# A graph network on one core: the block stage's loop on VectorE in another order, with two places per register load, and five moves around the last layer

## The reference

```
x = layernorm(x + L0(x, edges))          # h = x + sum of neighbours; relu(h W1 + b1) W2 + b2
x = layernorm(x + L1(x, src, dst))       # two layers of relu(h Ws + mean of neighbours Wn + b)
x = layernorm(x + L2(x, W, bias, edge_weight, src, dst))   # relu(segment_sum(edge_weight * (x W)[src], dst) + bias)
x = layernorm(x + L3(x, src, dst, edge_attr_20, edge_weight, edge_attr_3, ...))
```

## Time and profile before

| | us |
|---|---|
| median of 3 runs (2280.93 to 2287.22) | 2282.07 |
| the profiled execution's own time | 2290.75 |
| its span, first to last instruction | 2288.8 |
| block stage, first to last add | 396.1 to 707 |
| last product of L2 to first `filter_out` product | 1284 to 1317.8 |

### The profile page before, as it was taken

One profiled execution on the slowest core, in us unless ns is written; L12 is line 12 of the kernel. 1 busy time (PEld: TensorE's weight loads), 2 busy tenths in 40 slices (PEclk: granted clock), 3 DMA queues, 4 the chain that ended last, 5 costly groups with the idle time before them and its releaser, 6 DMA issues.

```text
span 2288.8 us, 37510 instructions
## 1 busy us (share of the span) xinstructions
PE 2078.5 (91%) x7867; PEld 1177.4 (51%) x7867; DVE 1595.2 (70%) x4611; ACT 1146.1 (50%) x3291; POOL 1237.1 (54%) x1526
## 2 busy tenths in 40 slices
PE   4787797888888999999999799999999999999987
PEld 3443343566664545455444555555555555555545
DVE  8976668898986070110413488888888888888886
ACT  0476456787872010000010366666666666666654
POOL 1477881000004888888886266666666666666541
PEclk9698798766668999999999899999999999999999
DMA  5410320000002121121121133333333333333321
GB/s 195 156 15 3 88 70 16 0 0 0 0 0 62 38 44 21 20 62 21 19 54 23 63 93 98 100 100 100 98 97 97 98 98 101 99 101 97 98 76 45
DMA packets 74566, 146.96 MB, mean 64 GB/s; under 512 B 26317, under 2 KB 37058, under 8 KB 74119
## 3 DMA queue, kind: packets, MB, share of 16 engines
q0 software_dynamic: 44192, 95.61, 16.9%
q1 hardware_dynamic: 28764, 47.76, 6.3%
q10 hardware_dynamic: 1538, 2.72, 0.3%
HBM read 123.11 MB, written 22.36 MB: 64 GB/s over the span
## 4 chain that ended last, share of the span: by engine, by line
PE 78%; DVE 13%; issue 4%; ACT 2%; DVEq 1%; another core or an unknown queue 1%; DMA 0%; ACTq 0%; POOL 0%; SPq 0%; POOLq 0%
PE ps L914 24%; PE ps L657 11%; PE ps L676 8%; PE ps L805 5%; PE ps L748 4%; PE ps L852 4%; PE ps L897 3%; PE ps L899 3%; PE ps L898 3%; PE ps L900 3%; DVE adj_t L1249 2%; PE ps L804 2%; PE ps L771 2%; DVE dense L1440 1%; DVE dense L1439 1%
## 5 line engine op out<-in xcount | busy, mean ns | idle before, releaser
L914 PE MATMUL ps<-adj_t 128*128 128x512 f32 x1288 | 614.7, 599 | 14.0 <-DVE adj_t L1677 14.0
L1132 ACT ACTIVATE adj_t<-adj_t 128x128 f32<-128x128 f32 x966 | 315.4, 389 | 210.0 <-DVE adj_t L1656 204.2
L590 POOL DMA_INDIRECT adj_t<-z_table,adj_t x322 | 310.5, 964 | 153.9 <-DVE adj_t L1666 68.3
L914 PEld LDWEIGHTS ps<-adj_t 128*128 128x128 f32 x1288 | 231.3, 189 | 248.7 <-issue 214.5
L548 POOL DMA_INDIRECT src_table<-st_two,src_rows x216 | 261.6, 1211 | 70.4 <-issue 65.2
L534 POOL DMA_INDIRECT pair_table<-dense x176 | 215.3, 1223 | 126.4 <-issue 115.8
L805 PE MATMUL ps<-dense 128*128 128x128 f32 x832 | 245.8, 414 | 0.0
L541 POOL DMA_DIRECT2D st_two<-records x54 | 31.9, 591 | 353.3 <-DVE adj_t L1464 353.1
L676 PE MATMUL ps<-wring,dense 128*128 128x512 f32 (+1 forms) x480 | 210.0, 600 | 4.5 <-issue 3.2
L897 PE MATMUL ps<-dense_r 128*128 128x512 f32 x322 | 200.2, 622 | 2.5 <-POOL dense_r L598 2.5
L1464 DVE TENSOR_TENSOR adj_t<-adj_t,ps 128x256 f32 x416 | 171.2, 411 | 30.8 <-issue 28.8
(11 more groups left out here) (285 smaller groups left out, 3775.0 us busy)
## 6 DMA issues: line engine op xcount, KB each, us to landing
src_table<-dense SPq DMA_DIRECT2D x8, 656.0 KB, 6.6
adj_t<-z_table,adj_t POOLq DMA_INDIRECT x322, 3.5
records<-dense SPq DMA_DIRECT2D x1, 5000.0 KB
adj_t<-src_table SPq DMA_DIRECT2D x73, 64.0 KB
adj_t<-zeros SPq DMA_DIRECT2D x1, 4576.0 KB
src_table<-st_two,src_rows POOLq DMA_INDIRECT x216
st_two<-records POOLq DMA_DIRECT2D x54, 62.5 KB
adj_t<-zeros SPq DMA_DIRECT2D x1, 3328.0 KB
```

Source lines behind the costliest of these rows:

```text
L590: g.indirect_dma_start(out=zg[:, s, c, :], out_offset=None, in_=z_table, in_offset=bass.IndirectOffsetOnAxis(ap=dsti[:, s, c:c + 1].bitcas ...
L914: last = mm(bank[6 + h], oh[:, c, :], msg[:, c, h * D:(h + 1) * D], start=c == c0, stop=c == c0 + count - 1)
L1132: last = A(msg[:, c, (2 + k) * P:(3 + k) * P], msg[:, c, MSG:MSG + P], ACT.Copy, scale=side[:, s, c, C_Y - ATT + k:C_Y - ATT + k + 1])
```

## The change

- Block stage on VectorE: `half` becomes `turn`. For each place the add comes first and the `select` for the chunk eight later behind it. Both waits (`blk_done`, `blk_added`) stand ahead of the add. A register load with two values comes ahead of the add of every even place, so four loads per turn of 8 places in place of one. The loop keeps its 50 turns.
- GpSimd clears `agg` when all ten tiles of `residual("l2_agg")` are done, not when the last product is.
- VectorE prepares L3's weights ahead of `residual("l2_agg")`; only the copy `identb` and the fill of `stat`, which lie in space that is still in use, stay behind it.
- ScalarE loads the table for exp and ln ahead of the copies of z.
- The ten stores of z are issued by SyncE, behind its record loads for the first two groups.
- GpSimd's `hidden_lo(0, 0)` stands behind two of the first four gathers, not behind all four.

```diff
@@ sync
             load_group(0, 0)
             load_group(0, 1)
+            for t in range(NT):
+                sp_eng.wait_ge(done["l3_z"], t + 1)
+                sp_eng.dma_start(z_table[t * P:t * P + rows_of(t), :], xb[0:rows_of(t), t, :]).then_inc(z_out, 16)
@@ gpsimd
-            pool.wait_ge(full, first["l2_agg"] + NT)
+            pool.wait_ge(done["l2_agg"], NT)
             g.memset(agg, 0.0).then_inc(agg_zero, 1)
             split(0, 0)
             split(0, 1)
-            for c in range(GROUP):
-                gather(0, 0, c)
+            gather(0, 0, 0)
+            gather(0, 0, 1)
             hidden_lo(0, 0)
+            gather(0, 0, 2)
+            gather(0, 0, 3)
@@ scalar
             copies_T("l3_xT")
+            nc.scalar.preload_act_table_set("natural_log_exp_and_others")
             for t in range(NT):
                 A(xb[0:r, t, :], taken("l3_z", t)[0:r, :], ACT.Copy).then_inc(done["l3_z"], 1)
-                act.wait_ge(done["l3_z"], t + 1)
-                act.dma_start(z_table[t * P:t * P + r, :], xb[0:r, t, :]).then_inc(z_out, 16)
...
             act.wait_ge(l3w_ready, 2)
-            nc.scalar.preload_act_table_set("natural_log_exp_and_others")
@@ vector, block stage
-            def half(i, h, first=False, last=False):
...
+            def turn(i, tail=False):
+                n0 = i * PLACES
+                for k in range(PLACES):
+                    c, n = k % (2 * AB), n0 + k
+                    if k % 2 == 0:
+                        _, block_at = nc.values_load_multi_w_load_instructions(
+                            pair_offs[0:1, ds(n, 2)], engines=[mybir.EngineType.DVE], min_val=0, max_val=AW_COLS - P, ...)
+                    dve.wait_ge(blk_done, n + 1)
+                    if not (isinstance(n, int) and n == 0):
+                        dve.wait_ge(blk_added, n)
+                    a = adj[:, :, ds(block_at[k % 2], P)]
+                    v.tensor_tensor(a, a, bank[c][:, 0:2 * P].rearrange("p (k n) -> p k n", k=2), ALU.add).then_inc(blk_added, 1)
+                    if not tail or k < PLACES - 2 * AB:
+                        select(n + 2 * AB, c)
+
+            for c in range(2 * AB):
+                select(c, c)
+            turn(0)
+            with dve.Fori(1, PAIR_CHUNKS // PLACES - 1) as i:
+                turn(i)
+            turn(PAIR_CHUNKS // PLACES - 1, tail=True)
@@ vector, towards L3
             residual("l1b_out", 48, relu=True)
-            residual("l2_agg", 64, relu=True)
...
-            link(v.tensor_copy(identb, ident[:, :]))
             row = pcol[0:PRODUCTS * ATT, :]
...
             link(v.scalar_tensor_tensor(bf2_r, bf2_r, ident[:, 0:1], bf2_lo, ALU.mult, ALU.add))
+            residual("l2_agg", 64, relu=True)
+            link(v.tensor_copy(identb, ident[:, :]))
             v.memset(stat, 1.0).then_inc(l3w_ready, 1)
```

More of the change, by code:

```diff
@@ L380, in build @@
         AB_IT = PAIR_CHUNKS // (2 * AB)
+        PLACES = 2 * AB
+        assert PAIR_CHUNKS % PLACES == 0
         L3_LOADS = 8 + 2 * PRODUCTS
@@ L1433, in _, with select @@
             dve.wait_ge(pair_merged, 3)
-            def select(i, c):
-                n = i * (2 * AB) + c
+            def select(n, c):
                 col = n * PAIR_COLS + PAIR_AT
@@ L1440, in select @@
                 v.tensor_scalar(sel_b[:, c, 1, :], iotab[:, :], dense[:, ds(col + 1, 1)], None, ALU.is_equal).then_inc(sel_ready, 1)
-            block_at = []
-            def half(i, h, first=False, last=False):
[L1446 to L1455, removed]
-                            skip_runtime_bounds_check_because="a sum of some of the steps between blocks; all of them make the last block's place")
[L1457 to L1478, removed]
+            def turn(i, tail=False):
[4 more added lines that the diff above has]
+                        _, block_at = nc.values_load_multi_w_load_instructions(
+                            pair_offs[0:1, ds(n, 2)], engines=[mybir.EngineType.DVE], min_val=0, max_val=AW_COLS - P,
+                            skip_runtime_bounds_check_because="a sum of some of the steps between blocks; all of them make the last block's place")
+                    dve.wait_ge(blk_done, n + 1)
[5 more added lines that the diff above has]
+                        select(n + 2 * AB, c)
```

## The result

Measured side by side on one chip, the kernel after takes 2360.55 us (median of 5 runs, 2354.93 to 2363.11), the kernel before 2284.74 (5 runs, 2280.93 to 2287.22). The ratio is 1.033, interval 1.0311 to 1.0349: slower by 76 us. The forecast was 2368, the range 2320 to 2402.

What follows compares the result with a forecast made beforehand. VectorE was taken to bound the block stage, its sequencer's time paid in full. +94 us for the loop, +2 for the turns outside and -10 behind L2 made +86: 2282 to 2368 us, range 2320 to 2402.

Steps and rivals of the forecast that it cites:

- Two take 0.30 + 0.04 = 0.34: Block stage, VectorE: a two-value register load takes 0.34 us, from one value at 0.30 and eight at 0.60.
- The load costs 0.82 - 0.16 = 0.66 us each turn. The branch costs 0.10 more: Block loop of the kernel before: of each turn's idle time the eight-value load costs 0.66 us, the branch 0.10.
- Each load costs 0.40: Block loop: each two-value load adds 0.40 us between S2, the step before the add, and the add.
- 0.15 for the waits: Block loop: the two waits ahead of the add cost 0.15 us at each of four even places, bounds 0 and 0.15.
- The branch, 0.37: Block loop: no longer beside the turn's last add, the branch costs 0.37 us a turn; lower bound 0.10.
- the 0.02 at odd places: Block loop: at the four odd places the waits cost 0.02 us each, bounds 0 and 0.05.
- TensorE under 70 of 100 us busy: Block stage, a sign to look for: TensorE under 70 of 100 us busy in the profile after.
- Behind L2, -10.4: From L2's end to L3's filter: the moves bring the first filter product 10.4 us earlier, bounds -12 and -5.
- A: Block stage: loads cost less than added, no extra wait instruction or a hidden branch; 2319 to 2352 us, chance 0.24.
- B: Block stage: loads have a floor, each costing what the eight-value one does; 2422 us, chance 0.07.
- C: Block stage: VectorE's sequencer runs ahead, loads and waits vanish under adds and selects; 2234 us, chance 0.07.
- D: Half-hidden loads, 0.1 us each, even out with the 10 us behind L2; 2275 to 2289 us, chance 0.02.

Runs made afterwards that it cites:

- run 1: Kernel after with one value per register load, so eight loads a turn: 2387.84 us, ratio 1.0448 to the kernel before.
- run 2: Kernel after with four values per register load, so two loads a turn: 2287.63 us, ratio 1.0014 to the kernel before.
- run 9: Kernel after, still four loads a turn, each loading four values of which two are used: 2363.87 us, ratio 1.0452 to the kernel before.
- run 10: Kernel after, still four loads a turn, each loading three values of which two are used: 2382.57 us, ratio 1.0533 to the kernel before.
- Run 4: Kernel after with the order and waits of the kernel before (select, load, add), still two values per load: 2336.73 us, ratio 1.0227 to the kernel before.
- run 3: Kernel after with the wait for the product moved ahead of the preceding `select`: 2335.77 us, ratio 1.0223 to the kernel before.
- run 7: Kernel before with only the late clearing and the early weights: 2272.19 us, ratio 0.9959 to the kernel before.
- run 8: Kernel before with only the late clearing, weights left behind the normalised tiles: 2283.24 us, ratio 1.0001 to the kernel before.
- Run 6: Kernel before with all five moves behind L2, block stage untouched: 2272.04 us, ratio 0.9958 to the kernel before.
- run 12: Kernel after with 32 places a turn, loads of four values, the order of the kernel before: 2233.34 us, ratio 0.9873 to the kernel before.

## Why the prediction was right, and where it was not

- **Direction, place and size: right.** +86 forecast on the profiled execution, +72.5 found; the slower time, the block stage as its place, four idle spells a turn with the one at the branch longest, 208 loads.
- **"Two take 0.30 + 0.04 = 0.34": wrong.** This is the term that failed, though the 0.53 lies inside its bounds of 0.30 and 0.60. A straight line was laid between one value and eight, but eight is two aligned fours. Measured 0.53, shown by the trace after; that the line between one and eight does not hold is shown by runs 1, 2, 9 and 10. By itself the true length would have added 4 x 0.19 x 50 = 38 us, which makes 2406 of the forecast, outside the range. That the forecast came so near is thus partly luck.
- **"The load costs 0.82 - 0.16 = 0.66 us each turn. The branch costs 0.10 more": wrong split.** Run 4 has, in the order of before, loads with the branch ahead of them and loads without: the branch costs 0.29, the load its own length less 0.12. The 0.76 of before is 0.48 for the load and 0.28 for the branch. "The sequencer is hardly one instruction ahead" described one place, not a rule: in the kernel after the load starts 0.12 us before S2.
- **"Each load costs 0.40", and 0.15 for the waits: right as a sum, by two errors that cancel.** The forecast from S2 to the add was 0.06 until the load starts, 0.34 for it, 0.31 behind it, 0.71 together. Measured: -0.12, 0.52, 0.29, together 0.69. The second wait ahead of the add costs 0.12 at an even place (runs 3 and 4) and 0 at an odd one, inside the bounds.
- **The branch, 0.37:** measured 0.30. That, and the 0.02 at odd places and at each load, make up the turn of 7.70 against 7.9, and with 50 turns most of the 85.5 against 96.
- **"TensorE under 70 of 100 us busy": wrong,** 76.7. There are 313 matmuls for 402; at the 0.211 us each of before they would fill 66 us. That they would run at 1.2 GHz from 415 us to the stage's end, and take 0.245, was not seen. It bounds nothing there: odd places still follow after 0.66 us.
- **Behind L2, -10.4: right,** -10.1. L1483 is never over 0.6 us, z runs at 0.91 us a tile at 2.4 GHz (forecast 0.85), the last copy ended 14.7 us behind L2's last tile (14), the filter came after 23.6 (24). Preparing the weights cost nothing, and "`identb`, then under the clearing, waits until 1296.3" did not come, for it ran just ahead of the clearing; nothing hung on it. Runs 7 and 8 add that the late clearing brings its gain only with the weights moved out of its way. Run 6, which has the moves alone, is 0.42% faster than before: the change contains a gain of 10 us and a loss of 85.
- **The rivals.** A (2319 to 2352) did not come: the EVENT_SEMAPHORE and the ALU_OP are there, and the branch is not hidden. B had some truth in that two values are dearer than the line says, but a floor it is not: one value takes 0.30 us and four 0.344. The Trainium skill's page "DMA: Bandwidth & Descriptors" (section "Latency and other measured facts") gives `tensor_load` about 600 ns at least; these loads from SBUF on VectorE go down to 0.297, so here the measurement decides against it. C (2234): the load starts only 0.12 us ahead of S2, not the 0.5 named, and nothing vanishes. The depth that the Trainium skill's page "TensorE: Matmul & The Clock Gate" (section "Architectural detail: the array is 16× 32×32, not 1× 128×128") gives for VectorE's queue does not show in this loop, whose sequencer waits for the last add once a place: its wait starts 0.04 us after that add's end at the places without a load. D did not come.

What stays open: what inside the load makes alignment to four matter is inferred from durations alone, and two places of run 12's turn are dearer than the sum. That each add's wait for the last is what keeps the sequencer close was not tried by itself, since without it the adds would race on `adj`.

## What to carry to other kernels

In a loop whose sequencer waits for its engine once per step, as this one does, price every register load, wait and branch as time on the path wherever it stands, and count them per turn; fewer and larger pieces win (longer turns, loads of four). Take the price of a load from a row with the same number of values and the same alignment; do not interpolate. When a long instruction of one engine blocks another, moving it only pays if what it would block at its new place is moved as well.

## What the runs showed of the hardware

- A register load from SBUF on VectorE took, by number of values: 1, 0.30 us; 2, 0.53; 3, 0.76; 4 beginning at a multiple of four, 0.344; 4 beginning at two above, 0.97; 8, 0.60; 16, 1.10. Loading two more values to use two made a turn 0.5 us longer; loading four at a multiple of four costs less than loading two.
- With two waits ahead of one instruction, one of them becomes an instruction of its own: x415 with both ahead of the add, none in the loop with one moved. Between the two kernels lie 0.12 us per load, though the record of that instruction shows 21 ns; an ALU_OP of 40 ns moved as well.
- The clearing by GpSimd held up two tensor_scalar steps of VectorE from SBUF to SBUF until about its end: 5.86 us for L1495, 8.74 for the weights' step L1588 of run 8. Two other steps from SBUF, L1506 and L1490, ran under it in their usual 0.69 us.
